# Two passes of attention scores moved from 96 and 98 partitions to 48 and 50, on opposite halves of TensorE's rows and alternating

## What is computed

```python
x = x + attn_a(layernorm(x)); x = x + ffn(layernorm(x))
x = x + attn_b(layernorm(x)); x = x + ffn(layernorm(x))

def attn_a(h):                       # 16 heads of 16 features
    Q, K, V = heads(h @ wq.T), heads(h @ wk.T), heads(h @ wv.T)
    Q, K = rotary(Q), rotary(K)
    scores = einsum('bhqd,bhkd->bhqk', Q, K) / 4     # only the first 25 and last 128 keys
    probs = softmax(scores)          # V gets a gated extra term from one token
    return heads_back(probs @ V) @ wo.T

def ffn(x):                          # 16 heads of 16 features, one shared key and value head
    gating = softmax(x @ W_gate.T); hot = one_hot(argmax(gating))
    q, k, v = split(x @ W_qkv.T)
    k_shared = sum_h(hot * k);  v_shared = sum_h(hot * max(gating) * v)
    att = softmax(causal(einsum('bhqd,bkd->bhqk', q, k_shared) / 4))
    return heads_back(att @ v_shared)
```

## Time and profile before

| | |
|---|---|
| median of 3 runs | 1037.86 us |
| lowest, highest | 1029.64, 1043.96 us |
| the profiled execution | 1040.56 us, its span 1038.8 us |
| mean granted TensorE clock | 0.955 |
| busy in the span: PE, PEld, DVE, ACT, POOL | 937.6, 739.5, 772.8, 533.8, 378.5 us |
| DMA | 53.72 MB, queues busy for 22.7% of 16 engines |

### The profile page before, as it was taken

How to read it: one execution, slowest core, us unless ns; L and a number is a source line. 1 busy time by engine, 2 the same in 40 slices (tenths; PEclk the granted TensorE clock), 3 DMA queues, 4 the chain that set the end, 5 groups by cost and what they waited for, 6 DMA issues and landing times.

```text
span 1038.8 us, 20288 instructions
## 1 busy us (share of the span) xinstructions
PE 937.6 (90%) x6656; PEld 739.5 (71%) x6656; DVE 772.8 (74%) x2461; ACT 533.8 (51%) x1379; POOL 378.5 (36%) x517
## 2 busy tenths in 40 slices
PE   2488899998998999988999999999999999899997
PEld 2377788887776677655778787787877777777763
DVE  6874688887878998656676767676677677988983
ACT  1113455555534455433565757575666574355555
POOL 1223788887753443334111010201011101244435
PEclk9665899999989999989999999999999999999999
DMA  6234344344222566400000000000000002333331
GB/s 202 63 63 62 75 84 81 81 87 92 60 48 50 113 149 137 96 2 1 1 1 1 1 1 2 1 2 1 2 1 1 1 2 62 79 79 92 76 84 33
DMA packets 59192, 53.72 MB, mean 52 GB/s; under 512 B 6592, under 2 KB 56144, under 8 KB 59088
## 3 DMA queue, kind: packets, MB, share of 16 engines
q1 hardware_dynamic: 59088, 52.41, 22.7%
HBM read 34.30 MB, written 17.30 MB: 50 GB/s over the span
## 4 chain that ended last, share of the span: by engine, by line
PE 40%; DVE 8%; issue 3%; ACT 0%; POOL 0%; DMA 0%; POOLq 0%; SPq 0%; DVEq 0%; ACTq 0%
PE bank L262 11%; PE bank L1803 7%; PE bank L1748 5%; PE bank L1736 4%; PE bank L1811 4%; PE bank L1570 2%; PE bank L1792 2%; PE bank L1582 2%; PE bank L1567 1%; DVE weights L1320 1%; DVE weights L1330 1%; DVE arena L1161 1%; PE bank L1608 1%; PE bank L1611 1%; PE bank L308 1%
## 5 line engine op out<-in xcount | busy, mean ns | idle before, releaser
L1161 DVE TENSOR_REDUCE arena<-bank 128x2 f32<-128x512 f32 (+1 forms) x192 | 128.9, 679 | 31.2 <-PE bank L1570 30.8
L802 ACT ACTIVATE weights<-bank 128x512 f32<-128x512 f32 x144 | 85.8, 597 | 120.1 <-PE bank L1582 119.2
L877 ACT ACTIVATE weights<-weights,neg_max 128x128 f32<-128x128 f32 (+1 forms) x256 | 113.7, 447 | 33.1 <-DVE neg_max L1320 33.1
L662 POOL TENSOR_SCALAR_AFFINE_SELECT weights<-weights 128x256 f32<-128x256 f32 x144 | 66.6, 463 | 135.5 <-ACT weights L802 135.3
L1803 PE MATMUL bank<-kbT,arena 128*128 128x128 f32 (+1 forms) x512 | 111.1, 340 | 1.1 <-DVE y L396 0.9
L1570 PE MATMUL bank<-kf_stack,q_stack 96*128 96x128 f32 (+1 forms) x512 | 110.8, 320 | 0.0
L618 POOL TENSOR_SCALAR weights<-weights 128x512 f32<-128x512 f32 x64 | 95.6, 1501 | 16.9 <-ACT weights L734 16.9
L884 ACT ACTIVATE weights<-bank 128x384 f32<-128x384 f32 x128 | 62.6, 489 | 52.1 <-PE bank L1811 51.9
L1320 DVE CUSTOM_DVE_ANT_0 weights<-bank,arena 128x128 f32<-128x128 f32 (+1 forms) x256 | 80.3, 351 | 11.8 <-PE bank L1803 9.9
L1330 DVE TENSOR_SCALAR weights<-weights,inv_sum 128x128 f32<-128x128 f32 (+1 forms) x256 | 84.1, 370 | 4.6
L689 POOL TENSOR_TENSOR arena<-rope,q_lo 128x512 f32<-128x512 f32 x32 | 41.0, 1282 | 114.9 <-DVE q_lo L1274 114.9
(11 more groups left out here) (215 smaller groups left out, 2553.9 us busy)
## 6 DMA issues: line engine op xcount, KB each, us to landing
q_stack<-scr_q SPq DMA_DIRECT2D x144, 128.0 KB, 3.7
scr_q<-q_hi SPq DMA_DIRECT2D x24, 256.0 KB, 2.3
scr_q<-q_lo SPq DMA_DIRECT2D x24, 256.0 KB, 2.5
ka_stack<-scr_k SPq DMA_DIRECT2D x48, 76.5 KB, 3.8
x_all<-x SPq DMA_DIRECT2D x8, 256.0 KB, 6.2
st_wo<-b_wo SPq DMA_DIRECT2D x8, 256.0 KB, 3.6
arena<-b_wqn SPq DMA_DIRECT2D x8, 256.0 KB, 3.8
out<-x_all SPq DMA_DIRECT2D x8, 256.0 KB, 2.2
```

What stands on the lines that cost most here:

```text
L877: last = a.activation(p, p, ACT.Exp, scale=-1.0, bias=neg_max[:, h % 4, t:t + 1], accum_out=sums[:, h % 4, t:t + 1])
L1161: v.tensor_reduce(into, p1[k % 2][:, :].rearrange("p (h k) -> p h k", h=n), AX.X, ALU.max, negate=True).then_inc(s["maxed"], 1)
```

## The change

Both stacks keep two copies of the 48 partitions: one at 0 to 47 for the first pass, one at 64 to 111 for the turned pass, with the shift rows at 112 and 113 (`STK, LOW, STK_F = 48, 64, 114`). The first pass multiplies over partitions 0 to 47, the turned pass over 64 to 113. Each fetch of `sp_get_q` and `get_k` becomes six DMAs in place of three, and PE waits for all six. In a, PE now issues scores of half t, then turned scores of half t, for t = 0 and 1; in f it issues the mask and the first head's scores, the turned scores, then the other heads' scores. The zero fills go; the -1 rows of `ka_stack` are filled by POOL at its start (18 partitions x 2560 elements, two stacks) with the padding zeroed by DVE in step (-2, 14); the shared key gets its second copy by one more POOL copy in `k48`, which is 114 columns wide.

```diff
-STK, STK_F = 96, 98
+STK, LOW, STK_F = 48, 64, 114
-N_FILLS, N_DVE_FILLS, N_STAGED = 7, 15, 25
+N_DVE_FILLS, N_STAGED = 10, 25
@@ sp_put_shift
-                row = STK + i
+                row = LOW + STK + i
@@ sp_get_q (get_k likewise; q_got and k_got count 96 in place of 48)
-            for row, hl in enumerate((0, 0, 1)):
-                sp.dma_start(q_stack[b % 2][row * HD:(row + 1) * HD, part, :].bitcast(f32),
-                             scr_q[hl].rearrange("(h d) t -> d h t", d=HD)[:, part, :]).then_inc(s[f"q_got{o}"], 16)
+            for lo in (0, LOW):
+                for row, hl in enumerate((0, 0, 1)):
+                    rows = slice(lo + row * HD, lo + (row + 1) * HD)
+                    sp.dma_start(q_stack[b % 2][rows, part, :].bitcast(f32),
+                                 scr_q[hl].rearrange("(h d) t -> d h t", d=HD)[:, part, :]).then_inc(s[f"q_got{o}"], 16)
@@ gpsimd, at its start
+            for stack in ka_stack:
+                g.memset(stack[96:STK_F, :, :].bitcast(f32), -1.0).then_inc(s_fill, 1)
+            pool.wait_ge(s_fill, 2)
@@ gpsimd, keys_of_f
+                    pool.wait_ge(*at(s, "k48", b, 3))
+                    g.tensor_copy(k48[:, :, LOW:LOW + STK], k48[:, :, 0:STK].bitcast(f32)).then_inc(s["k48"], 1)
@@ vector
-            def fill_stacks(i):
-                v.memset(q_stack[i][0:STK, :, :].bitcast(f32), 0.0).then_inc(s_fill, 1)
-                v.memset(ka_stack[i][0:STK, :, :].bitcast(f32), 0.0).then_inc(s_fill, 1)
+            def fill_pads():
+                dve.wait_ge(s_fill, 2)
+                for stack in ka_stack:
+                    v.memset(stack[0:STK_F, :, KA:KA_PAD].bitcast(f32), 0.0).then_inc(s_fill, 1)
-            def fill_shifts():
-                for stack in ka_stack:
-                    v.memset(stack[STK:STK_F, :, :].bitcast(f32), -1.0).then_inc(s_dfill, 1)
...
-            fill_stacks(0)
                 if (b, k) == (-2, 14):
+                    fill_pads()
                     fill_values()
-                if (b, k) == (-1, 4):
-                    fill_stacks(1)
-                    fill_shifts()
                 if (b, k) == (0, 1):
-                    for stack in kf_stack:
-                        v.memset(stack[0:STK, :].bitcast(f32), 0.0).then_inc(s_fill, 1)
                     fill_for_f()
@@ tensor, step_a (scores_a and scores_aT each issue one matmul a call)
-                if there(b):
-                    scores_a(b, k)
-                if there(b - 1):
-                    scores_aT(b - 1, k)
+                for i in range(2):
+                    if there(b):
+                        scores_a(b, k, i)
+                    if there(b - 1):
+                        scores_aT(b - 1, k, i)
@@ tensor, scores_aT and scores_T read partitions LOW to STK_F of both stacks
+                last = mm(p2[k % 2][rows, i * T:(i + 1) * T], ka_stack[b % 2][LOW:STK_F, h, keys],
+                          q_stack[b % 2][LOW:STK_F, h, :], start=True, stop=True)
@@ tensor, step of ffn (scores_f: mask and head 0 if first, else the other heads)
                     if there(b):
-                        scores_f(b, k)
+                        scores_f(b, k, True)
                     if there(b - 1):
                         scores_T(b - 1, k)
+                    if there(b):
+                        scores_f(b, k, False)
```

More of the change, by code:

```diff
@@ L105, in hybrid_layers_kernel @@
         y = sb("y", [P, NT, D])
-        k48 = sb("k48", [P, NT, 3 * HD], f32r)
+        k48 = sb("k48", [P, NT, STK_F], f32r)
         norm_bc = sb("norm_bc", [P, LORA])
@@ L127, in hybrid_layers_kernel @@
         s_w = sem("small_weights_loaded")
-        s_fill = sem("pool_fills_done")
+        s_fill = sem("stack_fills_done")
         s_dfill = sem("dve_fills_done")
@@ L496, in get_k @@
                 part = slice(o * OCT, (o + 1) * OCT)
-                for row, hl in enumerate((0, 1, 0)):
-                    sp.dma_start(ka_stack[b % 2][row * HD:(row + 1) * HD, part, 0:KA].bitcast(f32),
-                                 scr_k[hl].rearrange("(h d) t -> d h t", d=HD)[:, part, 0:KA])\
-                        .then_inc(sa[f"k_got{o}"], 16)
+                for lo in (0, LOW):
+                    for row, hl in enumerate((0, 1, 0)):
+                        rows = slice(lo + row * HD, lo + (row + 1) * HD)
+                        sp.dma_start(ka_stack[b % 2][rows, part, 0:KA].bitcast(f32),
+                                     scr_k[hl].rearrange("(h d) t -> d h t", d=HD)[:, part, 0:KA])\
+                            .then_inc(sa[f"k_got{o}"], 16)
             def step_a(b, k):
-                if (b, k) in ((-1, 8), (0, 8)):
-                    sp.wait_ge(s_fill, 2 if b < 0 else 4)
+                if (b, k) == (-1, 8):
+                    sp.wait_ge(s_fill, 4)
                 if k == 0 and there(b):
@@ L950, in fill_for_f @@
                     v.memset(m[:, :, :], 0.0).then_inc(s_dfill, 1)
-                for stack in kf_stack:
-                    v.memset(stack[STK:STK_F, :].bitcast(f32), 1.0).then_inc(s_dfill, 1)
+                v.memset(k48[:, :, STK:LOW].bitcast(f32), 0.0).then_inc(s_dfill, 1)
+                v.memset(k48[:, :, LOW + STK:STK_F].bitcast(f32), HD ** 0.5).then_inc(s_dfill, 1)
                 v.tensor_copy(ident_bf[:, :], ident).then_inc(s_dfill, 1)
@@ L1376, in _, with scores_a, scores_aT @@
             pe.wait_ge(s_id, 16)
-            def scores_a(b, k):
-                if k % OCT == 0:
-                    pe.wait_ge(*at(sa, f"q_got{k // OCT}", b, 48))
-                    pe.wait_ge(*at(sa, f"k_got{k // OCT}", b, 48))
-                pe.wait_ge(*at(sa, "maxed", b, k - 1))
-                for t in range(NT):
-                    last = mm(p1[k % 2][:, t * KA_PAD:t * KA_PAD + KA_EVEN], q_stack[b % 2][0:STK, k, t * P:(t + 1) * P],
-                              ka_stack[b % 2][0:STK, k, 0:KA_EVEN], start=True, stop=True)
-                last.then_inc(sa["s_ps"], 1)
-            def scores_aT(b, k):
+            def scores_a(b, k, t):
+                if t == 0:
+                    if k % OCT == 0:
+                        pe.wait_ge(*at(sa, f"q_got{k // OCT}", b, 96))
+                        pe.wait_ge(*at(sa, f"k_got{k // OCT}", b, 96))
+                    pe.wait_ge(*at(sa, "maxed", b, k - 1))
+                last = mm(p1[k % 2][:, t * KA_PAD:t * KA_PAD + KA_EVEN], q_stack[b % 2][0:STK, k, t * P:(t + 1) * P],
+                          ka_stack[b % 2][0:STK, k, 0:KA_EVEN], start=True, stop=True)
+                if t == NT - 1:
+                    last.then_inc(sa["s_ps"], 1)
+            def scores_aT(b, k, i):
                 o, j = k // OCT, k % OCT // 2
-                if k % OCT == 0:
-                    pe.wait_ge(*at(sa, f"shift{o}", b, 32))
-                pe.wait_ge(*at(sa, "exp", b, k - 1))
+                if i == 0:
+                    if k % OCT == 0:
+                        pe.wait_ge(*at(sa, f"shift{o}", b, 32))
+                    pe.wait_ge(*at(sa, "exp", b, k - 1))
                 rows, keys = (slice(0, P), slice(0, RB)) if k % 2 == 0 else (slice(0, VC), slice(RB, KA_PAD))
-                for i in range(2):
-                    h = o * OCT + i * G + j
-                    last = mm(p2[k % 2][rows, i * T:(i + 1) * T], ka_stack[b % 2][:, h, keys], q_stack[b % 2][:, h, :],
-                              start=True, stop=True)
-                last.then_inc(sa["sT_ps"], 1)
+                h = o * OCT + i * G + j
+                last = mm(p2[k % 2][rows, i * T:(i + 1) * T], ka_stack[b % 2][LOW:STK_F, h, keys],
+                          q_stack[b % 2][LOW:STK_F, h, :], start=True, stop=True)
+                if i == 1:
+                    last.then_inc(sa["sT_ps"], 1)
             def turn_maxima_a(b, o):
@@ L1572, in scores_f @@
                                   skip_group_check=True)
-                    last.then_inc(s["s_ps"], 1)
+                    if not first:
+                        last.then_inc(s["s_ps"], 1)
                 def scores_T(b, k):
```

43 lines of the change are left out of this document (19 added, 24 removed).

## The result

| | before | after |
|---|---|---|
| median of the runs | 1035.5 us | 1122.8 us (1119.75 to 1124.49) |
| ratio to before, 95% interval | 1 | 1.083 (1.075 to 1.092) |
| profiled execution / its span | 1040.6 / 1038.8 us | 1124.5 / 1122.7 us |
| DMA queue q1, share of 16 engines | 22.7% | 39.0% |

The changed kernel is slower by 8.3%. The direction was forecast. The size was not: 1070 us with a range to 1110 was forecast, and 1122.8 is 13 us above the range.

What follows compares the result with a forecast made beforehand. PE was taken to set the pace, DVE close behind. Fills -14, DMAs +21 and +2, halves and order +12 in a and +5 in f, clock +6: +32 on 1040.6 us, 1070 as a median, range 1030 to 1110.

Runs made afterwards that it cites:

- E1: Kernel before with six DMAs per fetch of the queries in place of three, all matmuls and order unchanged: 1088.3 us, ratio 1.044.
- E12: E1 with its added three DMAs cut from eight heads to four, 64 KB in place of 128: 1051.0 us, ratio 1.008.
- E5: Changed kernel with 16 useless full-width matmuls in PE's wait at every change of batch in a from the second batch on: 1086.8 us, ratio 1.047.
- E9: Kernel before with stack fills on POOL and useless matmuls in PE's waits for the first fetches of batches 0 to 3 of a: 1014.9 us, ratio 0.973.
- E7: Kernel before with its first pass over rows 0 to 47 alone, turned pass still at 98 rows, old order: 1121.0 us, ratio 1.079.
- E6: Changed kernel in the order of before, first-pass matmuls ahead of turned ones, halves and DMAs kept: 1117.2 us, ratio 1.078.

## What to carry to other kernels

A wait that more transfers make costs more than its length where TensorE's clock falls behind it. In the changed kernel the clock was low at or behind all eight changes of batch, in E1 at seven of eight. Where a change makes recurring waits like these of 3 us, price a fall at nearly every one of them, and not as a chance, with a length no shorter than the falls behind such waits that the trace already has (10 us here; it came to 7 to 24). Ask first whether the added bytes can be halved or moved off the wait (E12: half of the added bytes, four fifths of the loss gone), and try useless matmuls in the wait before anything is restructured. When a change bundles a cheap gain with a costly idea, price the gain alone: the fills on POOL were worth 1.3% in the old kernel.

## What the runs showed of the hardware beyond that

- Matmuls that compute nothing made a kernel 36 us faster (E5) and another 9 us (E9), by keeping TensorE at 2.4 GHz. PE was busy for 28.9 of 29.7 us in E5's batch from 198.0 us, and for 30.8 of 34.9 in the batch of after from 148.2.
- In E12 the stands of PE at the fourth and later changes of batch were 0.75, 0.64, 1.40, 0.62 and 2.46 us. The clock stayed up behind those of 0.6 to 0.75, and was low for 3.4 us behind the one of 1.40 and for 6.8 behind the one of 2.46. Stands of 3.2 to 3.9 brought it down for 7 to 24 us each time (E1, after). In between it was not the length alone: after E1's stand of 2.51 us the clock stayed up for 19 us, and after 2.69 us in after it was low for 13.6.
- DMAs of 128 KB issued 0.45 us apart on one queue land 1.0 us apart, those of 64 KB behind them 0.3 to 0.4.
- Into and out of half of the array with float32r matmuls costs 0.34 us together between full-width neighbours in a (0.26 on average over a batch), 0.36 in f (E7).
- A float32r matmul on the other half starts 0.01 us after the first one, ahead of a matmul that the code issues before it (E6).
- POOL fills 18 partitions x 2560 elements in 2.2 us, the time DVE takes for 96 or 2 partitions of as many.
